# First five turns of a fused vision and text kernel, written out in an order of their own

## The reference, cut to what matters

```
loc  = dwconv(gelu(conv(x, pl_w, stride=16)), pl_*)              # layer L
g    = gelu(conv(wavelet_packet(x), pg_w1)); g = gelu(dwconv(g, pg_*))   # layer G
glob = conv(g, pg_w2)                                            # layer W2
h = relu(dwconv(gate_mix(loc, glob), f1_*))                      # F1
h = relu(dwconv(h, f2_*)); h = dwconv(loc + h, f3_*)             # F2, F3
tokens = concat(cls, layernorm(h), txt)                          # 325 per image
q, k, v = mlp(layernorm(tokens), ...)     # two layers each, gelu between
y = windowed linear attention (span 64), layernorm, residual
out = y + quantized gated feed-forward (8-bit activations, ternary weights)
```

## Time and profile before

| what | us |
|---|---|
| three runs, median (lowest to highest) | 1143.92 (1141.91 to 1146.18) |
| profiled execution, its own time | 1147.13 |
| its span, first to last instruction | 1145.3 |
| PE busy | 1059.6 (93%) |
| DVE busy | 976.4 (85%) |
| ACT busy | 881.8 (77%) |
| POOL busy | 792.1 (69%) |
| mean granted clock of TensorE, as a share of full speed | 0.971 |

### The profile page before, as it was taken

The page is one execution under the profiler, slowest core; times in us unless marked ns, Lnnn a source line. Parts: engine busy times, 40 slices in busy tenths (PEclk is TensorE's granted clock), DMA queues, the critical chain, the costliest instruction groups (busy, mean ns, idle before and its releaser), DMA issues.

```text
span 1145.3 us, 19061 instructions
## 1 busy us (share of the span) xinstructions
PE 1059.6 (93%) x5641; PEld 700.3 (61%) x5691; DVE 976.4 (85%) x2829; ACT 881.8 (77%) x2173; POOL 792.1 (69%) x916
## 2 busy tenths in 40 slices
PE   6887999999999999999999999999999989888865
PEld 4554667666757575766666675757676666454522
DVE  0678868999989898999999998989899999666786
ACT  3446758697979888898979798988889787738545
POOL 4245475878787787878787778877787887646334
PEclk9888999999999999999999999999999999979988
DMA  8111010101001010101010100101010000000000
GB/s 342 43 50 40 4 50 4 50 5 58 13 22 49 11 59 10 60 11 60 7 61 5 33 38 19 51 10 60 11 60 10 18 9 12 8 16 16 16 16 22
DMA packets 23687, 41.14 MB, mean 36 GB/s; under 512 B 3649, under 2 KB 20385, under 8 KB 21281
## 3 DMA queue, kind: packets, MB, share of 16 engines
q1 hardware_dynamic: 23584, 39.93, 10.3%
HBM read 31.02 MB, written 7.99 MB: 34 GB/s over the span
## 4 chain that ended last, share of the span: by engine, by line
PE 53%; ACT 22%; DVE 16%; issue 4%; POOL 3%; DMA 2%; SPq 1%; DVEq 0%; POOLq 0%; ACTq 0%
PE bank L558 10%; PE bank L590 4%; ACT xh L1265 4%; PE bank L592 3%; PE bank L601 3%; PE bank L652 3%; ACT y_sb L1274 3%; DVE bank L1953 3%; PE bank L600 3%; ACT early L1251 2%; PE bank L776 2%; PE bank L536 2%; PE bank L708 2%; PE bank L537 2%; PE bank L654 2%
## 5 line engine op out<-in xcount | busy, mean ns | idle before, releaser
L1953 DVE SCALAR_TENSOR_TENSOR bank<-padA,c_col,bank 128x406 f32<-128x406 f32 x560 | 358.5, 640 | 9.1
L558 PE MATMUL bank<-x_sb,w_emb 128*128 128x392 f32 x576 | 221.1, 513 | 6.1 <-ACT padA L1201 3.1
L1251 ACT ACTIVATE prod<-padB,c_col 128x196 f32<-128x196 f32 x432 | 175.4, 451 | 4.9 <-DVE padB L1965 3.9
L558 PEld LDWEIGHTS bank<-x_sb,w_emb 128*128 128x128 f32 x576 | 102.0, 194 | 64.1 <-issue 12.6
L3045 POOL TENSOR_TENSOR yg<-y_f,c_gout 128x512 f32<-128x512 f32 (+2 forms) x73 | 92.9, 1273 | 52.5 <-DVE y_f L2234 52.2
L1251 ACT ACTIVATE early<-padB,c_col 128x196 f32<-128x196 f32 x288 | 118.9, 449 | 3.7 <-POOL accB L3079 3.6
L536 PE MATMUL bank<-accA,w_sq 128*128 128x196 f32 x256 | 66.5, 341 | 11.8 <-POOL accB L3079 6.8
L2214 DVE SCALAR_TENSOR_TENSOR ya<-th,bank 128x512 f32<-128x512 f32 (+2 forms) x73 | 49.9, 684 | 28.7 <-ACT th L1323 27.4
L708 PE MATMUL bank<-w_in,xq 128*128 128x512 bf16 (+2 forms) x252 | 67.1, 382 | 5.1 <-ACT xq L1317 2.4
L590 PE MATMUL bank<-xT,w_sq 128*128 128x325 f32 x192 | 64.4, 447 | 4.0 <-ACT hq L1209 3.9
L3064 POOL TENSOR_TENSOR prod<-prod 128x392 f32<-128x392 f32 x48 | 48.9, 1018 | 27.8 <-ACT prod L1251 27.7
(11 more groups left out here) (320 smaller groups left out, 3015.7 us busy)
## 6 DMA issues: line engine op xcount, KB each, us to landing
x_sb<-xt SPq DMA_DIRECT2D x16, 1176.0 KB, 5.2
out<-o_sb SPq DMA_DIRECT2D x64, 96.0 KB, 1.9
w_sq<-squares SPq DMA_DIRECT2D x1, 3840.0 KB, 15.9
h_sb<-txt SPq DMA_DIRECT2D x32, 51.8 KB
out<-o_sb SPq DMA_DIRECT2D x32, 48.0 KB, 1.9
h_sb<-txt SPq DMA_DIRECT2D x32, 44.2 KB
w_in<-win SPq DMA_DIRECT2D x1, 1024.0 KB, 17.8
h<-h SPq DMA_DIRECT2D x16, 48.0 KB, 1.9
```

Of the source, the lines that this page charges most:

```text
L558: done = mm(pE[:, 0:2 * N_PATCH], w_emb[:, k, m, :], x_sb[:, k, :], start=k == 0, stop=k == KC - 1)
L1251: made = go(grid(prod[ACC[s] ^ 1][:, k, :]), tap_view(padB[min(s, 2)], SIDE, k), ACT.Copy, scale=tapcol(s, 1, k))
L1953: v.scalar_tensor_tensor(grid(acc if k == TAPS - 1 else run), tap_view(pad, ROWS_A, k), tapcol(s, 0, k), grid(run), ALU.mult, ALU.add).the ...
```

## The change

Turns 0 to 4 are not run through `turn` any more: each engine gets a function `fill` with the same calls, each exactly once and with the same arguments, in a written-out order, and `all_turns` starts at turn 5. In PE's `fill` stand 30 calls of a matmul of the identity `c_id` with itself in nine groups (`keep_warm`), into bank 6 (pUP), which is first used in turn 6. What moves most in the orders:

- PE: `weight_totals` two places forward, ahead of the embed BB of pair 1; `query_key_weights` from ahead of embed GA of pair 1 to behind its LA; F1(0), G(1), W2(1), F2(0), L(1), F3(0) each four to seven places back behind embeds; F2(1) from ahead of the mlp of pair 0 to behind `mlp_wide` of key 1; F3(1) behind the last mlp part.
- ACT: `embed_out(0, GA)` ahead of products 4 to 8 of G(0); `mix_out(0)` behind seven products of G(1); `embed_out(1, LA)` ahead of all products of F1(0); `embed_out` of pairs 2 and 3, `input_norm` and `mlp_out` earlier among the products.
- DVE: `ternary_weights` between taps 5 and 6 of L(0); `query_key_blocks` from ahead of `mix(0)` to between taps 7 and 8 of F1(0); `token_biased` behind one tap of F1 instead of four; `input_bn(0)` three taps later.
- POOL: sums of L(1) between those of F1(0); the last sums of F1(1) ahead of `token_gain(0)`.
- SP: `load_txt` of pair 0 behind x of pair 3 and cls of pair 0; `load_txt(1)` behind x of pair 4.

In `drain` the wait for `emb_out` moves forward and the counts of `keep_busy` change.

```
-        def all_turns(turn, stop):
-            for it in range(stop):
+        def all_turns(turn, start, stop):
+            for it in range(start, stop):
...
+            def keep_warm(n):
+                for _ in range(n):
+                    mm(pUP[:, 0:P], c_id[:, :], c_id[:, :], start=True, stop=True)
...
+            def fill():                                  # PE
+                embed_chunk(0, EMB_BB, range(0, 2))
...
+                embed_chunk(0, EMB_LA, range(4, 6))
+                layer_G(0)
+                weight_totals()
+                embed_chunk(1, EMB_BB, range(0, 2))
+                embed_chunk(1, EMB_BB, range(2, 4))
+                embed_chunk(1, EMB_BB, range(4, 6))
+                layer_W2(0)
+                embed_chunk(1, EMB_GA, range(0, 2))
+                embed_chunk(1, EMB_GA, range(2, 4))
+                layer_L(0)
+                embed_chunk(1, EMB_GA, range(4, 6))
+                keep_warm(2)
+                embed_chunk(1, EMB_LA, range(0, 2))
+                embed_chunk(1, EMB_LA, range(2, 4))
+                embed_chunk(1, EMB_LA, range(4, 6))
+                query_key_weights()
+                embed_chunk(2, EMB_BB, range(0, 2))
+                keep_warm(1)
+                embed_chunk(2, EMB_BB, range(2, 4))
+                layer_F1(0)
+                embed_chunk(2, EMB_BB, range(4, 6))
+                layer_G(1)
+                embed_chunk(2, EMB_GA, range(0, 2))
+                layer_W2(1)
+                embed_chunk(2, EMB_GA, range(2, 4))
+                layer_F2(0)
+                embed_chunk(2, EMB_GA, range(4, 6))
+                keep_warm(4)
+                embed_chunk(2, EMB_LA, range(0, 2))
+                embed_chunk(2, EMB_LA, range(2, 4))
+                layer_L(1)
+                embed_chunk(2, EMB_LA, range(4, 6))
+                keep_warm(2)
+                layer_F3(0)
+                keep_warm(9)
+                embed_chunk(3, EMB_BB, range(0, 2))
+                keep_warm(6)
+                layer_F1(1)
+                embed_chunk(3, EMB_BB, range(2, 4))
+                layer_G(2)
+                embed_chunk(3, EMB_BB, range(4, 6))
+                layer_W2(2)
+                embed_chunk(3, EMB_GA, range(0, 2))
+                embed_chunk(3, EMB_GA, range(2, 4))
+                transposes(0, 0)
+                transposes(0, 1)
+                keep_warm(3)
+                transposes(0, 2)
+                keep_warm(2)
+                mlp_wide(0, 'qw1', U_Q1, xT)
+                mlp_half(0, 'qw1', U_Q1, xT)
+                mlp_wide(0, 'kw1', U_K1, xT)
+                layer_F2(1)
+                embed_chunk(3, EMB_GA, range(4, 6))
+                mlp_half(0, 'kw1', U_K1, xT)
+                layer_L(2)
+                mlp_wide(0, 'vw1', U_V1, xT)
+                keep_warm(1)
+                mlp_half(0, 'vw1', U_V1, xT)
+                mlp_wide(0, 'kw2', U_K2, hk)
+                mlp_half(0, 'kw2', U_K2, hk)
+                layer_F3(1)
...
                 layer_W2(15)                             # PE, drain
                 transposes(13, 0)
+                pe.wait_ge(emb_out, PAIRS * EMBS)
+                keep_busy(1)
                 transposes(13, 1)
+                keep_busy(2)
                 transposes(13, 2)
+                keep_busy(1)
                 layer_F2(14)
                 rounded_hidden_transposes(11, 1)
                 mlp_wide(13, 'qw1', U_Q1, xT)
+                keep_busy(1)
...
+                keep_busy(1)                             # ahead of layer_F3(14)
...
-                pe.wait_ge(emb_out, PAIRS * EMBS)
...
+            def fill():                                  # ACT, its beginning
+                embed_out(0, EMB_BB)
+                products(0, G_, range(0, 1))
+                products(0, G_, range(1, 2))
+                products(0, G_, range(2, 3))
+                products(0, G_, range(3, 4))
+                embed_out(0, EMB_GA)
+                products(0, G_, range(4, 5))
...
-            all_turns(turn, 17)
+            fill()
+            all_turns(turn, 5, 17)
             drain()
```

More of the change, by code:

```diff
@@ L1041, in drain @@
                 rounded_hidden_transposes(12, 2)
-                keep_busy(4)
+                keep_busy(2)
                 ffn_out(12, 2)
@@ L1103, in drain @@
                 ffn_out(14, 0)
-                keep_busy(2)
+                keep_busy(1)
                 rounded_token_transposes(14, 2)
@@ L1153, in drain @@
                 ffn_in(15, 5)
-                keep_busy(9)
+                keep_busy(10)
                 rounded_hidden_transposes(15, 3)
@@ L3026, in _ @@
             assert gsteps[0] == GATE_STEPS
-            all_turns(turn, 16)
+            fill()
+            all_turns(turn, 5, 16)
             drain()
```

441 lines of the change are left out of this document (438 added, 3 removed).

## The result

| | before | after |
|---|---|---|
| median of runs (lowest to highest), us | 1142.91 (1141.54 to 1146.18, 4 runs) | 1156.43 (1154.87 to 1159.71, 4 runs) |
| ratio to before, 95% interval | | 1.0122 [1.0092, 1.0153] |
| profiled execution, its span, us | 1147.13, 1145.3 | 1159.71, 1157.9 |
| mean granted clock | 0.971 | 0.970 |

The changed kernel is 13.5 us (1.2%) slower, clear of the 0.5%; 1142 was forecast, and the range ended at 1150. The profiled execution is the slowest of its four. To find the place I cut each profiled execution at three points that every kernel of this case has: PE's first embed, PE's start on embed LA of pair 3 (the first work of turn 5, so the end of the fill), and the issue of x of pair 5. From there on the orders are the same until the drain. Each kernel has one profiled execution, so each stretch is read once per kernel.

What follows compares the result with a forecast made beforehand. PE was taken to bound the kernel. The fill would end 1.5 us earlier with the clock lost at 38, 3.0 if kept; 2.0 was taken, other terms 0: 1141.9 from the median 1143.9, called 1142, range 1135 to 1150.

Steps and rivals of the forecast that it cites:

- What bounds the kernel: Whole kernel: PE is busy 93% of the span, so reaching turn 5 earlier moves the end by nearly as much.
- ACT's first embed, weight_totals, L(0), mix(0): Early fill: the first embed's move costs 3.6 us on ACT, 2.75 on DVE; mix(0) still starts 11.7 us earlier.
- The key/query product: Inside F1(0): DVE waits 1.7 and 4.5 us (second wait's bounds 0 to 9.0); of 11.7 us gained 1.1 remain.
- rival B: Fill: half clock from the gap at 35.7 and the key/query product's weight loads stays; slower, 1152 us; chance 0.13.
- To layer F1(1): Fill, from DVE's mix(0) on: F1(1) starts at 111.2 against 116.02, 4.8 us earlier, and runs at half clock.
- The mlp stretch: End of the fill: mlp_wide of q starts about 129.9 against 133.09; PE ends at about 154.9, or 153.4 with clock held.
- SP: Load queue in the fill: txt of pair 0 behind x of pair 3 and cls, 5 us of DMA needed at 117; 0.
- keep_warm: PE in the fill: 30 calls, at most 0.32 us each, 9.6 in all if nothing hid them; taken as 0.
- rival D: Turn 5: DVE's wait for F2(1) puts it 2 us behind and eats the gain, 1144 to 1145; 0.58, forecast included.
- The drain: End of the kernel: keep_busy changes, 6 more early and 3 fewer net later; 0, bounds -0.8 to +1.4 us.
- rival C: Drain: another phase saves say 5 us of the half clock from 1007.8 to 1024.4, giving 1137 us; chance 0.07.

Runs made afterwards that it cites:

- e7: e1 with layer F2(1) and ACT's products for it ahead of the mlp of pair 0, mix_out(2) behind the input norms; 1145.3 us, ratio 1.0011.
- e5: e1 with ACT's embed_out(0, GA) again behind product 8 of G(0); 1149.0 us, ratio 1.0037.
- e6: e1 with PE's second half of the key/query product behind embed(2, BB) and DVE's last copies behind the taps of G(1); 1150.7 us, ratio 1.0062.
- e1: The changed kernel with SP's loads of the first five turns ordered as before the change; 1148.5 us, ratio 1.0039.
- e10: The changed kernel with txt of pair 0 loaded ahead of cls of pair 0, still behind x of pair 3; 1151.9 us, ratio 1.0071.
- e3: e1 with the 30 keep_warm calls taken out; 1153.7 us, ratio 1.0057.
- e14: e13 with DVE's order from mix(2) to the end of the fill as before the change; 1144.0 us, ratio 0.9990.
- e12: e9 with only DVE's last copies of the key/query product moved, behind tap 4 of G(1); 1142.9 us, ratio 0.9993.
- e13: e9 with F3(1) on PE ahead of mlp_half of key 2, as before the change; 1141.8 us, ratio 0.9974.
- e4: The changed kernel with the drain of before the change; 1162.6 us, ratio 1.0154.
- e11: e9 with the drain of before the change; 1147.7 us, ratio 1.0038.
- e9: e1 with both e5's move of ACT's first embed and e7's move of F2(1); 1142.3 us, ratio 0.9987.
- e8: The kernel before the change with only the new drain; 1144.1 us, ratio 0.9998.

## Why the prediction was wrong, by its steps

*What bounds the kernel.* Right up to the drain: PE passes on what the fill loses. +7.4 us in the fill are seen at x(5) in full, with 6.8 us on top, and from x(5) to x(15) every kernel takes the same time to 0.6 us. The end does not follow so well: e7 comes to x(5) 209.3 us behind its first embed and has 1145.3, e5 comes at 206.0 and has 1149.0.

*ACT's first embed, weight_totals, L(0), mix(0).* Right in size: `weight_totals` at 38.50 (39.15), L(0) at 51.00 (51.2), `mix(0)` at 54.56 (54.6), the clock at 0.50 from 34 us on, behind the gap of 2.0 us at 30.5 already (forecast: behind the next, at 38). The prediction's readings of the clock in the kernel before are some tenths off as well: it fell at 48.6 and 113.4, not 48.8 and 113.7, and was back at 1024.7, not 1024.4; no term hangs on that. e5 shows that the move of `embed_out(0, GA)` costs 4.35 us of the fill. I had priced that as a part of the 11.7 us gain and did not ask what L(0) would gain without it.

*The key/query product.* The waits were forecast at 1.7 and 4.5 us and are 1.97 and 6.57. The clock held through the first eight matmuls of the second half and fell in the 20 one-column ones (0.95 at 67, 0.50 at 68 us in the windows of 1 us), so the half that I took for a full clock ran slow for its second part. This is between my value and the bound of 9.0, and rival B's mechanism in small. Here a gap of 1.50 us, ahead of 64.58, stands 3.4 us before the fall, so this trace alone doesn't say whether the gap or the one-column matmuls did it. e6 does: PE is idle for the last time ahead of 68.58 and works without a hole from there, the clock is back at 72.3, and it falls at 79.2, at the end of the same 20 one-column matmuls. The Trainium skill, "TensorE: Matmul & The Clock Gate", section "Why this matters for your kernels", says that TensorE kept busy continuously gets the full clock; the trace of e6 disagrees. The windows of the changed kernel, then PE's timeline and the windows of e6 (the granted clock is the third number from the right, PE's busy us the second number):

```profile
67.00:68.00 1.00, 1.00 (x8) 0.95 (x7) 0.00 (x0) 0.00 (x0) 1.00 (x2) 0.95 0.00 0
68.00:69.00 1.00, 1.00 (x5) 0.97 (x5) 0.00 (x0) 0.00 (x0) 1.00 (x2) 0.50 0.00 0
```

```profile
68.58 0.67 PE L547 MATMUL bank<-accA,w_sq 128*128 128x196 f32 x2 [2.26 <-POOL accB L3521]
...
75.95 1.31 PE L818 MATMUL bank<-c_col,r 128*128 128x1 f32 x8
```

```profile
78.00:79.00 1.00, 1.00 (x8) 0.95 (x8) 0.00 (x0) 0.00 (x0) 0.00 (x0) 1.00 0.00 0
79.00:80.00 1.00, 1.00 (x5) 0.99 (x5) 0.80 (x4) 0.00 (x0) 0.00 (x0) 0.58 0.00 0
```

*To layer F1(1).* 113.72 instead of 111.2. The missing 2.1 us of the product are most of it; half clock at F1(1) and F3(0) at full clock were as forecast.

*The mlp stretch.* The step said that nm_a and rs_a would be there 0.4 us later than before. With the loads in order (e1) nm_a is done at 126.1, where before had 122.7: 3.4 us later, not 0.4. `mlp_wide` of q starts at 133.61 against 129.9 forecast and 133.09 before, its second matmuls at half clock from 133.8 to 137. The 3 us that F1(1) was late and the clock lost in the transposes' waits (0.50 at 134 to 136 us in e1) are what is missing; I had followed the clock up to F1(1) and no further. With SP's order as changed the wait of 4.59 us for txt comes on top, and `mlp_wide` of q starts at 136.86.

*SP.* This is the step that failed: "on SP the txt load of pair 0 goes behind x of pair 3 and cls: 5 us of DMA, needed at 117", costed at 0. I took the time of the transfer and its deadline, and did not ask when SP would come to the instruction. `load_cls` ahead of it waits for POOL's last `token_add`, until 117.4, and DVE comes to `input_bn` at 121.1: a lead of under 4 us for a load that was issued at 118.0 and for which DVE stood until 125.7. The lead of 42 us that the load had (75 against 117) was its cover. And I counted only pair 0; txt and cls of pair 1 behind x of pair 4 cost another 3.4 us (e10 to e1). Together 7.9 us in these orders and 12.5 us in the old ones. With this term the forecast of 1142 would have been 1149.9. The 6.5 us that are then left to 1156.4, the same as from 1142 to e1's 1148.5, come from the other steps of this list; the range, up to 1150, would have held e1.

*keep_warm.* Costed at 0, and the fill shows 0 within the scatter of 1.5 us (e3). It does not hold the clock ahead of F1(1): the six calls there fill 1.5 us, PE then stands 3.83 us, and F1(1) runs at half clock, as forecast. Behind the other groups PE waits at most 1.1 us.

*Turn 5.* I had rival D cost 2 us and put it down to the wait for F2(1). The size was right (2.4 us) by luck, the place wrong: taking 7.6 us from that wait (e7) left the stretch at 66.08; DVE's order around the wait for F3(1) was it (e14).

*The drain.* Costed at 0 with a rival C of 5 us for the clock's phase. The changed kernel lost nothing there (301.2 us from x(15) to the end against 302.0), but across the kernels this is the largest term after SP's: 297.1 to 303.9 us, with the same orders up to the drain. The profiled executions of e7, e12 and e13 have 297, those of e4 and e11, with the old drain, 303.5 to 303.9.

The sum, by the landmark that all kernels share, x(5) counted from the first embed: the kernel before has 204.2 us and the changed one 218.4. Taking SP's order back gives 8.1 (e1, 210.3), ACT's first embed 4.35 more (e5, 206.0), F2(1) 1.3 (e9, 204.7), F3(1) and DVE's tail 2.1 (e14, 202.6). So without these losses the new orders come to x(5) 1.6 us earlier than the profiled execution of before, and 0.2 us earlier than e8, which has the orders of before up to the drain. The steps were taken out one after the other, each seen in one profiled execution, and the times don't follow them to the last us: the clock in the drain moves by as much.

## What to carry to other kernels

When a load is moved on a queue, look at the instruction that it lands behind: behind a load that waits for a computed value, every load starts only after that wait, however early its data were free. Put large loads without a wait ahead of small ones with one. And a step forward for one layer is worth only what the engine that serves it next can take: DVE's stall moved to its next waits, for ACT and PE (e12), and the `mix(0)` that came 11.7 us early became 0.5 to 2 us at the end of the fill (e9).
